# Starting the first layer norm inside the output projection, slice by slice, in a post-norm transformer layer on 8 cores

## The chip, the cores and the metric

The kernel runs on all 8 cores of one Trainium2 chip. Every core runs the same program on its own data (half of the tokens of one of four sequences) and nothing is exchanged between cores. The metric is the device time in microseconds of the slowest core. TensorE is the matrix engine (PE in the profile, PEld its weight loads), VectorE is DVE, ScalarE is ACT, GpSimd is POOL, SyncE is SP.

## The reference

One transformer layer with layer norms after the residual sums:

```
x = layernorm(x + attention(x, Wq, Wk, Wv, Wo))        # causal, 16 heads of 64, D = 1024
x = layernorm(x + down(silu(gate(x)) * up(x)))         # hidden 3072, int weights / 127
layernorm(v) = (v - mean(v)) / sqrt(var(v) + 1e-5)     # over the 1024 features
```

The input is 4 sequences of 4096 tokens with 1024 features in float32.

## The kernel before

Each core owns 2048 tokens (`TOWN`). Activations lie transposed: the 1024 features are `NCH` = 8 chunks of 128 partitions, the tokens are columns. `y` is the float32 tile of 128 x (8 x 2048) that holds the residual stream. Work on it goes by *slice* `s` (`NQS` = 4 slices of 512 tokens) and by chunk (`ncx` or `m`, 0 to 7).

The kernel has stages one after the other: attention with its projections; the output projection Wo; the first layer norm; the feed-forward part; the second layer norm; one store of `y`. A barrier of all engines stands behind attention, behind the first layer norm and behind the second.

**Output projection.** A list `wo_iters` has 32 entries (chunk outside, slice inside). For each, TensorE runs 8 matmuls of 128x512 (line 642) into one of two PSUM tiles `wps`, and VectorE adds the residual `xres` and writes `y` (line 649, called the eviction here). The matmuls of an entry wait until the eviction two entries back has emptied their tile. SyncE loads `xres` four entries ahead. Behind the list TensorE and ScalarE wait for the last eviction, the PSUM of the projection is given back and that of the layer norm is taken: `stp`, two pairs of 1x512 sums, and `bc2`, two pairs of 128x512 broadcasts.

**Layer norm** (`ln_stats_and_apply`, used for both norms). `stats(s)` does for each chunk a Square on ScalarE (line 555, y to bf16 `ysq`), a cast on VectorE (line 559, y to bf16 `ybf`) and two matmuls against a column of ones (lines 563 and 565), which add the sums over features into `stp`. `ysq` and `ybf` have two buffers each. Behind that, for each slice, comes a chain on one-partition rows: Square on ScalarE (579), variance on VectorE (583), Ln and Exp on ScalarE (587, 590), the shift on VectorE (593), then float32 matmuls that spread scale and shift over 128 partitions into `bc2` (598, 600). Then the *apply*: 8 multiplications and 8 additions on VectorE (607, 609), in place in `y`. `stats(0)` and `stats(1)` go first; `stats(s + 2)` is issued behind the apply of slice s, and its matmuls wait for it, since both use the same `stp` pair.

Every engine takes its instructions in the order in which the program issues them, so the order of these calls is the order on each engine. What matters of it here is, in the projection, the wait of the matmuls for `wps`, and in the layer norm:

```
for s in range(min(2, NQS)):
    stats(s)
for s in range(NQS):
    ...chain and apply of slice s...
    if s + 2 < NQS:
        stats(s + 2)
```

Of the kernel before, what the change touches and what calls it, by code (L numbers as in the profile page):

```python
# [8 lines left out]
F32 = mybir.dt.float32  # L9
# [4 lines left out]
ALU = mybir.AluOpType  # L14
# [17 lines left out]
class Sem:  # L32
    def __init__(self, stack, nc, name):
        self.h = stack.enter_context(nc.semaphore(name))
        self.n = 0
# [7 lines left out]
def build_program(cfg):  # L43
    D, NH, DH, HID, T = cfg["D"], cfg["NH"], cfg["DH"], cfg["HID"], cfg["T"]
    NCH = D // 128
    NHC = HID // 128
    NB = T // 128
    TOWN = T // 2
    NBANK = TOWN // 512
    NKVS = T // 512  # L50
    NQS = TOWN // 512
# [8 lines left out]
    nc = bass.Bass("TRN2", target_bir_lowering=False, num_devices=1)  # L60
# [22 lines left out]
    with st:  # L83
        consts = st.enter_context(nc.sbuf_tensor("consts", [128, 4], F32))
        ones_col_bf = st.enter_context(nc.sbuf_tensor("ones_col_bf", [128, 1], BF16))
        ones_row_f = st.enter_context(nc.sbuf_tensor("ones_row_f", [1, 128], F32))
# [12 lines left out]
        s_evV = Sem(st, nc, "s_evV")  # L99
# [16 lines left out]
        s_lnA = Sem(st, nc, "s_lnA")  # L116
        s_lnV = Sem(st, nc, "s_lnV")
        s_lnP = Sem(st, nc, "s_lnP")
# [397 lines left out]
        if debug:  # L516
# [4 lines left out]
        y = st.enter_context(nc.sbuf_tensor("y", [128, NCH * TOWN], F32))  # L521
# [7 lines left out]
        ysq = [ph_b.enter_context(nc.sbuf_tensor(f"ysq{i}", [128, 512], BF16))  # L529
               for i in range(2)]  # L530
        ybf = [ph_b.enter_context(nc.sbuf_tensor(f"ybf{i}", [128, 512], BF16))
               for i in range(2)]
        rows = ph_b.enter_context(nc.sbuf_tensor("rows", [1, 6 * 512], F32))
# [3 lines left out]
            woT.rearrange("(c p) n -> p c n", p=128)), 16)  # L537
        wo_ready = s_wo.n

        def ln_stats_and_apply(stp, bc2, ysq, ybf, rows, sA, sV, sP):  # L540
            ysq_free = [0, 0]
            ybf_free = [0, 0]
            stats_done = [0, 0]
            bc_done = [0, 0]
            apply_done = [0, 0]
            rows_free = 0

            def stats(s):
                sb = s % 2
                q0 = s * 512  # L550
                nc.tensor.wait_ge(sV.h, apply_done[sb])
                for m in range(NCH):
                    bi = m % 2
                    nc.scalar.wait_ge(sP.h, ysq_free[bi])
                    sA.inc(nc.scalar.activation(  # L555
                        ysq[bi][:, :], y[:, m * TOWN + q0: m * TOWN + q0 + 512],
                        AF.Square))
                    nc.vector.wait_ge(sP.h, ybf_free[bi])
                    sV.inc(nc.vector.tensor_copy(
                        ybf[bi][:, :], y[:, m * TOWN + q0: m * TOWN + q0 + 512]))  # L560
                    nc.tensor.wait_ge(sA.h, sA.n)
                    nc.tensor.wait_ge(sV.h, sV.n)
                    nc.tensor.matmul(stp[sb][0][:, :], ones_col_bf[:, :], ybf[bi][:, :],  # L563
                                     start=(m == 0), stop=(m == NCH - 1))
                    sP.inc(nc.tensor.matmul(  # L565
                        stp[sb][1][:, :], ones_col_bf[:, :], ysq[bi][:, :],
                        start=(m == 0), stop=(m == NCH - 1)))
                    ysq_free[bi] = sP.n
                    ybf_free[bi] = sP.n
                stats_done[sb] = sP.n  # L570

            for s in range(min(2, NQS)):
                stats(s)
            for s in range(NQS):
                sb = s % 2
                q0 = s * 512
                nc.scalar.wait_ge(sP.h, stats_done[sb])
                nc.scalar.wait_ge(sP.h, rows_free)
                sA.inc(nc.scalar.activation(rows[:, 0:512], stp[sb][0][:, :],
                                            AF.Square, scale=1.0 / D))  # L580
                nc.vector.wait_ge(sA.h, sA.n)
                nc.vector.wait_ge(sP.h, stats_done[sb])
                sV.inc(nc.vector.scalar_tensor_tensor(  # L583
                    rows[:, 1536:2048], stp[sb][1][:, :], 1.0 / D, rows[:, 0:512],
                    op0=ALU.mult, op1=ALU.subtract))
                nc.scalar.wait_ge(sV.h, sV.n)
                sA.inc(nc.scalar.activation(rows[:, 2048:2560], rows[:, 1536:2048],
                                            AF.Ln, bias=float(cfg["EPS"])))
                nc.scalar.wait_ge(sA.h, sA.n)
                sA.inc(nc.scalar.activation(rows[:, 2048:2560], rows[:, 2048:2560],  # L590
                                            AF.Exp, scale=-0.5))
                nc.vector.wait_ge(sA.h, sA.n)
                sV.inc(nc.vector.scalar_tensor_tensor(  # L593
                    rows[:, 2560:3072], stp[sb][0][:, :], -1.0 / D, rows[:, 2048:2560],
                    op0=ALU.mult, op1=ALU.mult))
                nc.tensor.wait_ge(sV.h, sV.n)
                nc.tensor.wait_ge(sV.h, apply_done[sb])
                nc.tensor.matmul(bc2[sb][0][:, :], ones_row_f[:, :], rows[:, 2048:2560],  # L598
                                 start=True, stop=True)
                sP.inc(nc.tensor.matmul(bc2[sb][1][:, :], ones_row_f[:, :],  # L600
                                        rows[:, 2560:3072], start=True, stop=True))
                bc_done[sb] = sP.n
                rows_free = sP.n
                nc.vector.wait_ge(sP.h, bc_done[sb])
                for m in range(NCH):
                    yv = y[:, m * TOWN + q0: m * TOWN + q0 + 512]
                    sV.inc(nc.vector.tensor_mul(yv, yv, bc2[sb][0][:, :]))  # L607
                    nc.vector.wait_ge(sV.h, sV.n)
                    sV.inc(nc.vector.tensor_add(yv, yv, bc2[sb][1][:, :]))  # L609
                apply_done[sb] = sV.n  # L610
                if s + 2 < NQS:
                    stats(s + 2)
            nc.tensor.wait_ge(sV.h, sV.n)
            nc.scalar.wait_ge(sV.h, sV.n)

        wo_iters = [(ncx, s) for ncx in range(NCH) for s in range(NQS)]
        wps_free = [0, 0]
        xr_free = [0, 0, 0, 0]
        xr_done = [0, 0, 0, 0]
# [13 lines left out]
        for idx, (ncx, s) in enumerate(wo_iters):  # L633
            q0 = s * 512
            i = idx % 2
            j = idx % 4
# [4 lines left out]
            for kcx in range(NCH):  # L641
# [3 lines left out]
                    start=(kcx == 0), stop=(kcx == NCH - 1))  # L645
# [6 lines left out]
            xr_free[j] = s_evV.n  # L652
            if idx + 4 < len(wo_iters):
                issue_xres(idx + 4)
        nc.tensor.wait_ge(s_evV.h, s_evV.n)
        nc.scalar.wait_ge(s_evV.h, s_evV.n)
        ofm_st.close()
        wo_ps.close()
        ln_ps = ExitStack()
        stp = [[ln_ps.enter_context(nc.psum_tensor(f"stp{i}_{j}", [1, 512], F32))  # L660
                for j in range(2)] for i in range(2)]
        bc2 = [[ln_ps.enter_context(nc.psum_tensor(f"bc2{i}_{j}", [128, 512], F32))
                for j in range(2)] for i in range(2)]
        ln_stats_and_apply(stp, bc2, ysq, ybf, rows, s_lnA, s_lnV, s_lnP)
        ln_ps.close()
        ph_b.close()
        nc.all_engine_barrier()
        if debug:
# [35 lines left out]
        for fs in range(NFS):  # L704
# [11 lines left out]
            for hc in range(NHC):  # L716
# [12 lines left out]
                for nh in range(NH2):  # L729
# [3 lines left out]
                    for m in range(NCH):  # L733
# [3 lines left out]
                            start=(m == 0), stop=(m == NCH - 1))  # L737
# [4 lines left out]
                    for m in range(NCH):  # L742
# [3 lines left out]
                            start=(m == 0), stop=(m == NCH - 1))  # L746
# [16 lines left out]
            for dc in range(NCH):  # L763
                for nh in range(NH2):
                    c0 = nh * 512
                    i = (dc * NH2 + nh) % 2
                    nc.tensor.wait_ge(s_fdve.h, dps_free[i])
                    last = None
                    for hc in range(NHC):
# [3 lines left out]
                            start=(hc == 0), stop=(hc == NHC - 1))  # L773
                    s_fpe.inc(last)
                    nc.vector.wait_ge(s_fpe.h, s_fpe.n)
                    yv = y[:, dc * TOWN + t0 + c0: dc * TOWN + t0 + c0 + 512]
                    s_fdve.inc(nc.vector.scalar_tensor_tensor(
                        yv, dps[i][:, :], cfg["QSCALE"], yv,
                        op0=ALU.mult, op1=ALU.add))
# [6 lines left out]
        stpc = [[ln_ps2.enter_context(nc.psum_tensor(f"stc{i}_{j}", [1, 512], F32))  # L786
                 for j in range(2)] for i in range(2)]
        bcc = [[ln_ps2.enter_context(nc.psum_tensor(f"bcc{i}_{j}", [128, 512], F32))
                for j in range(2)] for i in range(2)]
        ysq2 = [ph_c.enter_context(nc.sbuf_tensor(f"ysq2{i}", [128, 512], BF16))  # L790
                for i in range(2)]
        ybf2 = [ph_c.enter_context(nc.sbuf_tensor(f"ybf2{i}", [128, 512], BF16))
                for i in range(2)]
        rows2 = ph_c.enter_context(nc.sbuf_tensor("rows2", [1, 6 * 512], F32))
        ln_stats_and_apply(stpc, bcc, ysq2, ybf2, rows2, s_lnA, s_lnV, s_lnP)
        ln_ps2.close()
        ph_c.close()
        nc.all_engine_barrier()
# [66 lines left out]
```

## Time and profile before

| | us |
|---|---|
| median of 2 runs (2127.88 to 2134.34) | 2131.11 |
| the profiled execution, its time | 2126.39 |
| its span, slowest core (core 4) | 2125.3 |
| spans of the 8 cores | 2107.4 to 2125.3 |
| mean granted TensorE clock of the cores | 0.844 to 0.852 of full |

Busy time in the span of 2125.3 us: TensorE 1614.1 us (76%), ScalarE 797.8 us (38%), VectorE 641.1 us (30%), GpSimd 162.4 us (8%). How to read the rows of a timeline: start in us, duration in us (of the whole merged stretch where a count above 1 stands behind), engine, line, operation, output from input, count, and in brackets how long the engine was idle before and which instruction released it. PEclk is the granted TensorE clock as a share of 2.4 GHz; 0.50 is 1.2 GHz.

### The profile page before, as it was taken

The page shows a single profiled execution, that of the slowest core. Times are in us where ns is not written, and L with a number is a line of the kernel's source. Part 1 is how long each engine was busy: PE and PEld are TensorE (multiplying, and loading weights), DVE is VectorE, ACT ScalarE, POOL GpSimd, SP SyncE. Part 2 cuts the span into 40 slices and gives each one's busy share as a digit, 9 for nine tenths or more (in the row PEclk, how much of TensorE's full clock was granted, in tenths as well). Part 3 has the DMA queues.
Part 4 walks back from the last instruction along what each step waited for, and adds up shares of the span by engine and source line. Part 5 has one row for each costly group of instructions (what it writes and reads, how often), then busy time and mean ns, then how long its engine had stood idle before and what let it go on. Part 6 is the DMA issues. An engine that isn't in the chain of part 4 may idle for free. (4 is left out here: it accounts for less than half of the span.)

```text
span 2125.3 us, 22768 instructions; the slowest of 8 cores (2107.4 to 2125.3 us)
## 1 busy us (share of the span) xinstructions
PE 1614.1 (76%) x7146; PEld 618.6 (29%) x7240; DVE 641.1 (30%) x1500; ACT 797.8 (38%) x935; POOL 162.4 (8%) x205
## 2 busy tenths in 40 slices
PE   3858988789887788885776749524699989999830
PEld 1513333133332233321211114101244434444300
DVE  1333242532423533325213123562111121111254
ACT  0025766667663566644485810310111001110220
POOL 1010000000001000010000010002122002220000
PEclk9968999789996799975696859857899999999965
DMA  7791324523250622320000025008878207870004
GB/s 100 109 129 21 54 47 60 67 44 60 41 80 3 88 43 41 61 41 3 1 1 1 1 49 137 15 0 113 95 70 80 21 0 70 80 70 1 1 0 158
DMA packets 173633, 109.02 MB, mean 51 GB/s; under 512 B 102574, under 2 KB 164016, under 8 KB 172496
## 3 DMA queue, kind: packets, MB, share of 16 engines
q0 software_dynamic: 167744, 90.65, 33.2%
q1 hardware_dynamic: 5776, 16.91, 2.6%
q8 instruction: 65, 1.06, 0.2%
q14 instruction: 48, 0.39, 0.1%
HBM read 189.07 MB, written 8.65 MB: 93 GB/s over the span
## 5 line engine op out<-in xcount | busy, mean ns | idle before, releaser
L415 ACT ACTIVATE pt<-sp,cbias 128x1024 bf16<-128x1024 f32 (+3 forms) x640 | 622.6, 985 | 364.9 <-PE sp L403 353.6
L443 PE MATMUL op<-pt,vbuf 128*65 128x512 bf16 (+3 forms) x1280 | 378.7, 381 | 124.9 <-DVE pt L424 55.3
L398 PE MATMUL sp<-qbuf,kbuf 64*128 64x512 bf16 (+3 forms) x640 | 239.4, 383 | 2.1 <-DVE cbias L324 2.1
L403 PE MATMUL sp<-qbuf,kbuf 64*128 64x512 bf16 (+3 forms) x640 | 239.6, 383 | 0.0
L734 PE MATMUL gps<-x1b,wgb 128*128 128x512 bf16 x752 | 185.8, 388 | 65.1 <-DMA wub<-wuT 57.2
L751 ACT ACTIVATE sgb<-gps 128x512 bf16<-128x512 f32 x96 | 57.3, 597 | 420.8 <-PE gps L734 420.8
L443 PEld LDWEIGHTS op<-pt,vbuf 128*65 128x65 bf16 x1280 | 121.8, 117 | 267.6 <-issue 224.2
L743 PE MATMUL ups<-x1b,wub 128*128 128x512 bf16 x753 | 182.8, 384 | 0.8
L226 PE MATMUL pp<-xstg,wkb 128*128 128x512 bf16 x481 | 145.4, 416 | 45.6 <-DMA xstg<-xfm 40.0
L770 PE MATMUL dps<-hbuf,wdb 128*128 128x512 bf16 x752 | 165.2, 379 | 3.1 <-DVE hbuf L755 2.3
L240 PE MATMUL pp<-wvb,xstg 128*128 128x256 bf16 x1024 | 163.2, 280 | 0.6
L755 DVE TENSOR_TENSOR hbuf<-sgb,ups 128x512 bf16<-128x512 bf16 x96 | 66.0, 688 | 319.9 <-PE ups L743 319.9
L398 PEld LDWEIGHTS sp<-qbuf,kbuf 64*128 64x128 bf16 x640 | 58.4, 94 | 252.5 <-issue 250.4
L734 PEld LDWEIGHTS gps<-x1b,wgb 128*128 128x128 bf16 x768 | 74.1, 99 | 164.9 <-issue 84.4
L555 ACT ACTIVATE ysq<-y 128x512 bf16<-128x512 f32 x64 | 38.6, 625 | 179.4 <-DVE y L649 104.3
L421 DVE TENSOR_TENSOR pt<-pt,mka 128x128 bf16<-128x128 bf16 x128 | 28.7, 224 | 249.7 <-ACT pt L415 248.2
L743 PEld LDWEIGHTS ups<-x1b,wub 128*128 128x128 bf16 x768 | 76.1, 99 | 94.0 <-issue 5.8
L770 PEld LDWEIGHTS dps<-hbuf,wdb 128*128 128x128 bf16 x768 | 74.9, 98 | 93.4 <-issue 3.2
L297 ACT ACTIVATE qsq<-kbuf 128x512 bf16<-128x512 bf16 x64 | 39.5, 627 | 161.4 <-DVE qbuf L272 138.9
L240 PEld LDWEIGHTS pp<-wvb,xstg 128*128 128x128 bf16 x1024 | 81.2, 98 | 59.0 <-issue 43.9
L252 DVE CAST vbuf<-pp 128x256 bf16<-128x256 f32 x128 | 54.4, 425 | 138.9 <-PE pp L240 138.3
L264 PE MATMUL pp<-xstg,wqb 128*128 128x512 bf16 x246 | 74.1, 420 | 24.7 <-DMA xstg<-xq 24.1
(89 smaller groups left out, 1187.3 us busy)
## 6 DMA issues: line engine op xcount, KB each, us to landing
xstg<-xfm POOLq DMA_DIRECT2D x32, 1024.0 KB, 9.1
xstg<-xq POOLq DMA_DIRECT2D x16, 1024.0 KB, 8.4
wgb<-wgT POOLq DMA_DIRECT2D x48, 256.0 KB, 4.5
wub<-wuT POOLq DMA_DIRECT2D x48, 256.0 KB, 5.3
xres<-xq SPq DMA_DIRECT2D x32, 256.0 KB, 3.8
yout<-y SPq DMA_DIRECT2D x1, 8192.0 KB, 23.4
wdb<-wdT POOLq DMA_DIRECT2D x1, 6144.0 KB, 44.2
wqb<-wqT POOLq DMA_DIRECT2D x4, 512.0 KB, 7.7
```

The source lines that it names most:

```text
L226: return nc.tensor.matmul(ps[:, 0:512], wkb[pb][:, m * PD + nk * 128: m * PD + nk * 128 + 128], xs[:, m * 512:(m + 1) * 512], start=(m == ...
L240: return nc.tensor.matmul(ps[:, 0:PD], xs[:, m * 512 + jb * 128: m * 512 + jb * 128 + 128], wvb[pb][:, m * PD:(m + 1) * PD], start=(m == 0 ...
L264: return nc.tensor.matmul(ps[:, 0:512], wqb[pb][:, m * PD + nq * 128: m * PD + nq * 128 + 128], xs[:, m * 512:(m + 1) * 512], start=(m == ...
L398: nc.tensor.matmul(sp[buf][:, js * 128: 512], kbuf[pb][0:64, hp * T + kb * 128: hp * T + kb * 128 + 128], qbuf[pb][0:64, hp * TOWN + qbase ...
L403: s_s.inc(nc.tensor.matmul(sp[buf][:, 512 + js * 128: 1024], kbuf[pb][64:128, hp * T + kb * 128: hp * T + kb * 128 + 128], qbuf[pb][64:128 ...
L415: s_exp.inc(nc.scalar.activation(pview, sview, AF.Exp, bias=cbias[pb][:, 0:1]))
L443: lastpv = nc.tensor.matmul(ops[hl][:, js * 128: 512], vbuf[pb][:, kb * VGW + (2 * hp + hl) * 65: kb * VGW + (2 * hp + hl) * 65 + 65], pt[ ...
L734: lastg = nc.tensor.matmul(gps[:, :], wgb[wi][:, m * 128:(m + 1) * 128], x1b[:, m * FFS + c0: m * FFS + c0 + 512], start=(m == 0), stop=(m ...
L743: last = nc.tensor.matmul(ups[:, :], wub[wi][:, m * 128:(m + 1) * 128], x1b[:, m * FFS + c0: m * FFS + c0 + 512], start=(m == 0), stop=(m ...
L751: s_fact.inc(nc.scalar.activation(sgb[:, :], gps[:, :], AF.Silu))
L755: s_fdve.inc(nc.vector.tensor_mul(hbuf[:, hc * FFS + c0: hc * FFS + c0 + 512], sgb[:, :], ups[:, :]))
L770: last = nc.tensor.matmul(dps[i][:, :], wdb[:, hc * D + dc * 128: hc * D + dc * 128 + 128], hbuf[:, hc * FFS + c0: hc * FFS + c0 + 512], s ...
```

## The change

The layer norm helper becomes a class `LN` with two methods, `stats(s)` and `finish(s)` (the chain and the apply of one slice), so that its calls can be placed among other work.

- The list of the output projection now has the slice outside and the chunk inside. When the 8 chunks of slice s are done, the program issues `stats(s)` and, from s = 1 on, `finish(s - 1)`; behind the list comes `finish(3)`.
- The PSUM of the first layer norm is taken ahead of the projection, beside `wps`: two `stp` pairs as before, but one `bc2` pair in place of two. The waits for a free `stp` and a free `bc2` are kept apart (`apply_st`, `apply_bc`).
- In `stats`, ScalarE waits for the slice's last eviction (`ready_of`).
- In `stats`, in both layer norms, the cast to `ybf` goes from VectorE to ScalarE (`nc.scalar.copy`), behind the Square of the same chunk.
- The second layer norm has the old order of calls, written out, and both its `bc` pairs.

```diff
             def stats(self, s):
-                nc.tensor.wait_ge(sV.h, apply_done[sb])
+                nc.tensor.wait_ge(sV.h, self.apply_st[sb])
+                if self.ready_of is not None:
+                    sem, val = self.ready_of(s)
+                    nc.scalar.wait_ge(sem.h, val)
                 for m in range(NCH):
                     bi = m % 2
...
-                    nc.vector.wait_ge(sP.h, ybf_free[bi])
-                    sV.inc(nc.vector.tensor_copy(
-                        ybf[bi][:, :], y[:, m * TOWN + q0: m * TOWN + q0 + 512]))
+                    nc.scalar.wait_ge(sP.h, self.ybf_free[bi])
+                    sA.inc(nc.scalar.copy(
+                        self.ybf[bi][:, :], y[:, m * TOWN + q0: m * TOWN + q0 + 512]))
                     nc.tensor.wait_ge(sA.h, sA.n)
-                    nc.tensor.wait_ge(sV.h, sV.n)
...
+        bc2 = [[ln_ps.enter_context(nc.psum_tensor(f"bc2{i}_{j}", [128, 512], F32))
+                for j in range(2)] for i in range(1)]
...
-        wo_iters = [(ncx, s) for ncx in range(NCH) for s in range(NQS)]
+        wo_iters = [(ncx, s) for s in range(NQS) for ncx in range(NCH)]
...
             if idx + 4 < len(wo_iters):
                 issue_xres(idx + 4)
-        nc.tensor.wait_ge(s_evV.h, s_evV.n)
-        nc.scalar.wait_ge(s_evV.h, s_evV.n)
+            if ncx == NCH - 1:
+                y_slice_done[s] = s_evV.n
+                ln1.stats(s)
+                if s >= 1:
+                    ln1.finish(s - 1)
+        ln1.finish(NQS - 1)
...
+        ln2 = LN(stpc, bcc, ysq2, ybf2, rows2, s_lnA, s_lnV, s_lnP)
+        for s in range(min(2, NQS)):
+            ln2.stats(s)
+        for s in range(NQS):
+            ln2.finish(s)
+            if s + 2 < NQS:
+                ln2.stats(s + 2)
```

## Rows read from the trace of the kernel before

**Rows 1.** Stages by windows: us, busy (instructions) of each engine, PEclk, DMA share, GB/s

```profile
1279.60:1337.20 57.60, 56.49 (x250) 25.24 (x254) 22.08 (x33) 0.00 (x0) 0.00 (x0) 0.97 0.51 128
1337.20:1436.40 99.20, 35.22 (x80) 7.79 (x80) 60.00 (x105) 25.91 (x44) 0.00 (x0) 0.64 0.00 0
...
2002.00:2101.50 99.50, 35.23 (x80) 7.59 (x80) 60.07 (x105) 27.63 (x45) 0.00 (x0) 0.64 0.00 0
```

**Rows 2.** Groups by line, 1279.6 to 1437 us: busy, mean ns, idle before, releaser

```profile
L649 DVE TENSOR_TENSOR y<-wps,xres 128x512 f32<-128x512 f32 x32 | 22.1, 692 | 53.2 <-PE wps L642 53.2
...
L555 ACT ACTIVATE ysq<-y 128x512 bf16<-128x512 f32 x32 | 19.1, 624 | 141.8 <-DVE y L649 104.3 <-PE stp L565 37.4
```

**Rows 3.** Timeline, evictions 8 and 32, and the first stats operations behind the last

```profile
1295.13 0.69 DVE L649 TENSOR_TENSOR y<-wps,xres 128x512 f32<-128x512 f32 x1 [1.04 <-PE wps L642]
...
1336.57 0.69 DVE L649 TENSOR_TENSOR y<-wps,xres 128x512 f32<-128x512 f32 x1 [1.03 <-PE wps L642]
1337.18 0.75 DVE L559 CAST ybf<-y 128x512 bf16<-128x512 f32 x2
1337.41 1.15 ACT L555 ACTIVATE ysq<-y 128x512 bf16<-128x512 f32 x2 [104.29 <-DVE y L649]
...
1338.29 0.38 PE L563 MATMUL stp<-ybf,ones_col_bf 128*1 128x512 bf16 x1 [1.90 <-ACT ysq L555]
...
1338.50 0.38 PE L565 MATMUL stp<-ysq,ones_col_bf 128*1 128x512 bf16 x1
...
1338.98 1.15 ACT L555 ACTIVATE ysq<-y 128x512 bf16<-128x512 f32 x2 [0.42 <-PE stp L565]
```

**Rows 4.** Timeline, slice 0: its chain, its apply and the apply's end

```profile
1349.48 0.57 ACT L579 ACTIVATE rows<-stp 1x512 f32<-1x512 f32 x1
...
1350.23 0.68 DVE L583 SCALAR_TENSOR_TENSOR rows<-stp,rows 1x512 f32<-1x512 f32 x1 [0.85 <-ACT rows L579]
...
1354.32 1.76 PE L600 MATMUL bc<-rows,ones_row_f 1*128 1x512 f32 x2
...
1356.19 0.69 DVE L607 TENSOR_TENSOR y<-y,bc 128x512 f32<-128x512 f32 x1 [3.06 <-PE bc L600]
...
1367.31 0.76 DVE L559 CAST ybf<-y 128x512 bf16<-128x512 f32 x2
```

**Rows 5.** TensorE in 4 us windows: us, busy (instructions), PEclk, DMA share, GB/s

```profile
1280.00:1284.00 4.00, 4.00 (x14) 0.65 0.00 0
1284.00:1288.00 4.00, 4.00 (x20) 1.00 0.43 85
...
1352.00:1356.00 4.00, 2.62 (x4) 0.81 0.00 0
...
1368.00:1372.00 4.00, 3.72 (x9) 0.56 0.00 0
```

**Rows 6.** Timeline, slices 1 and 3 of the first layer norm

```profile
1366.71 0.69 DVE L609 TENSOR_TENSOR y<-y,bc 128x512 f32<-128x512 f32 x1
...
1373.89 0.57 ACT L579 ACTIVATE rows<-stp 1x512 f32<-1x512 f32 x1
...
1418.16 0.67 DVE L583 SCALAR_TENSOR_TENSOR rows<-stp,rows 1x512 f32<-1x512 f32 x1
...
1425.16 0.69 DVE L607 TENSOR_TENSOR y<-y,bc 128x512 f32<-128x512 f32 x1 [4.11 <-PE bc L600]
...
1435.68 0.69 DVE L609 TENSOR_TENSOR y<-y,bc 128x512 f32<-128x512 f32 x1
```

**Rows 7.** Timeline, the second layer norm: first Square, first row operation, first apply

```profile
2003.51 1.15 ACT L555 ACTIVATE ysq<-y 128x512 bf16<-128x512 f32 x2
...
2016.38 0.57 ACT L579 ACTIVATE rows<-stc 1x512 f32<-1x512 f32 x1
...
2024.13 0.69 DVE L607 TENSOR_TENSOR y<-y,bcc 128x512 f32<-128x512 f32 x1 [4.11 <-PE bcc L600]
```

**Rows 8.** One line's instructions: the loads of activation tables

```profile
L28 ACT ACT_TABLE_LOAD  x3: 1283/1283/1283, 1.1 to 2002.2; - x3
```

## What was predicted before the changed kernel ran

> **What bounds the kernel now.** I read the page first (TensorE is busy for three quarters of the span), then the busy time by stage, and then only the two stages that the change touches, in the groups by line and the timeline. The reader is to see three things. The projection with its evictions lasts 57 us and TensorE is busy nearly all of it [rows 1]; the evictions wait for matmuls 53.2 us of it [rows 2]. They come every (1336.57 - 1295.13) / 24 = 1.727 us [rows 3], a group of eight matmuls at 2.4 GHz. The two layer norms last 99 us each, and no engine is busy for more than 60 of them [rows 1]: they are chains through three engines. And TensorE's clock: it is at the upper level while Wo runs, at 1.2 GHz in the first microseconds of it, when TensorE had been idle before, and it falls again when TensorE has little to do in the layer norm [rows 5]. The aim of such an overlap would be to run the norm's 99 us under the projection. VectorE has the room. The question is the order on TensorE.
>
> **Part 1, the slice boundary.** All engines take the calls in order, so the next slice's Wo matmuls stand on TensorE's queue behind `stats(s)` and, from s = 1, behind the broadcast matmuls of `finish(s - 1)`. TensorE itself waits at each boundary.
>
> - From the last eviction's start to the first Square: 1337.41 - 1336.57 = 0.84 us [rows 3].
> - Square and copy now alternate on ScalarE. No row has the copy; I price it as a Square. Two of these take 1.15 us [rows 3], one 0.63 [rows 2], so the second starts 0.52 behind the first, and a chunk costs 1.04. With two buffers, chunk m + 2 also waits for chunk m's matmuls: 1.15 for both operations, 0.25 until the matmul (1338.29 behind a Square's end at 1337.41 + 0.63), 0.21 + 0.38 for both matmuls, 0.10 to the next Square (1338.98) [rows 3]: 2.09 us for two chunks, about the same as ScalarE's own 2.08. At 1.2 GHz both matmuls take 1.05 in place of 0.59: 2.55 us.
> - Eight chunks up to the next free place on ScalarE: 3 x 2.09 + 2.08 = 8.35 us, or 3 x 2.55 + 2.08 = 9.7. I take 9.0. TensorE is free after 6.27 + 1.04 + 1.15 + 0.25 + 0.43 = 9.1 us, or 10.9. I take 10.0, in the middle, since TensorE is busy for 0.43 of 1.04 us here, and rows show either clock beside such shares [rows 5].
> - From the row Square to the first apply operation: 1356.19 - 1349.48 = 6.7 us [rows 4], 2024.13 - 2016.38 = 7.75 at 1.2 GHz [rows 7]. I take 7.2. The broadcast ends as the apply begins (1354.32 + 1.76 = 1356.08) [rows 4], so TensorE is held as long.
>
> **Part 2, Wo behind an apply.** For slices 2 and 3 VectorE has an apply in its queue ahead of the evictions: 1367.31 - 1356.19 = 11.1 us [rows 4]. TensorE can fill its two `wps` tiles in 3.5 us, or 6.9 at 1.2 GHz, and then stands until the first eviction is over. I take 11.1, then 0.9 (an eviction of 0.69 [rows 2] and a handover of 0.2), a third group at 1.2 GHz with its last matmul 3.0 us behind its first, five groups at 1.727 (8.6), and 0.57 to its eviction: 24.2 us from the first apply operation to the slice's last eviction. Without the apply ahead (slice 1) it is 7 x 1.727 + 2.1 = 14.2, plus 1.7 for one group at half clock, 15.9.
>
> **The sum of projection and first norm**, starts in the clock of the profiled execution:
>
> - last eviction of slice 0 at 1295.1 [rows 3], Square at 1296.0, TensorE free at 1306.0;
> - last eviction of slice 1 at 1321.8, Square 1322.7, rows of slice 0 at 1331.7, apply(0) from 1338.9;
> - last eviction of slice 2 at 1363.1, Square 1363.9, rows 1372.9, apply(1) from 1380.1;
> - last eviction of slice 3 at 1404.3, Square 1405.2, rows 1414.2, apply(2) from 1421.4;
> - `finish(3)`: its variance stands behind apply(2) on VectorE as it does now: 1421.4 + 11.1 = 1432.5, then 7.0 to the apply (1425.16 - 1418.16) and 11.2 for it (1435.68 + 0.69 - 1425.16) [rows 6]: 1450.7.
>
> It now ends at 1436.4, so this part costs 14.4 us more. With every unknown at 2.4 GHz (9.1, 8.35, 6.7, no slow group, 6.0 in `finish(3)` by 1356.19 - 1350.23 [rows 4]) it ends at 1440.7, +4.3. With all at 1.2 GHz (10.9, 9.7, 7.8, two slow groups behind an apply) it ends at 1458.9, +22.5. The order of the `xres` loads costs nothing: they are of the same size, four entries ahead, and an entry never gets shorter. The single `bc2` pair costs nothing: the broadcast of slice s always comes behind the apply of s - 1 by the order on VectorE.
>
> **Part 3, the second norm.** Only the copies move. The first 16 chunks now take 2016.38 - 2003.51 = 12.9 us [rows 7]; with both operations on ScalarE 7 x 2.09 + 2.08 = 16.7, or 19.9 at 1.2 GHz: +3.8 to +7.1, I take 5.4. For slices 2 and 3 two chunks lie ready before the apply ends, but the other six do not: from the apply's end (1366.71 + 0.69) to the row Square it is now 6.5 us [rows 6], the same in both norms; with the change 1.4 to the third Square, then 2 x 2.09 + 2.08: 7.6, or 8.5. That is +1.1 to +2.0, I take 1.6, twice. The second norm: +8.6, bounds +6.1 and +11.2.
>
> The copy goes to the slower engine: two casts on VectorE take 0.75 us, one starting about 0.32 behind the other, against 0.52 on ScalarE [rows 3], and VectorE is idle in exactly these stretches. The Trainium skill, "ScalarE: Activation LUTs", section "Rules for kernel authors", speaks against such a move too: it gives simple elementwise work to VectorE. By it, with the casts left on VectorE, the second norm would add nothing and the first would save 32 x (1.04 - 0.75), 9 us, where 0.75 is a chunk now, (1349.48 - 1337.41) / 16 [rows 3, 4]; the sum would be some 18 us lower than mine, near 2132.
>
> **Everything else** is untouched, and all 8 cores do the same. The feed-forward part starts its weight loads behind the barrier, so it moves as a block.
>
> **The sum.** 14.4 + 8.6 = +23.0 us on the profiled execution's 2126.4: 2149.4 us. The median of the two runs is 4.7 us above the profiled one. I say 2150. Bounds: +10.4 and +33.7, so 2136.8 to 2160.1.
>
> **Rivals.**
>
> 1. *TensorE's order does not bind* (faster). If the next slice's Wo matmuls ran while the stats matmuls wait, the projection would end at 1336.6 as now, with the applies of slices 0 and 1 in VectorE's gaps, and behind it would come 0.8 + 9.0 + 7.2 + 11.1 + 7.0 + 11.2 = 46 us: 1383, 53 earlier, with the second norm's +8.6 a time of 2082. It decides if more than two thirds of TensorE's waits at the boundaries vanish. Against it: no row shows a matmul ahead of one issued before it. Chance 1%.
> 2. *TensorE never gets back to full clock in slices 1 to 3* (slower). 24 groups at 3.45 in place of 1.727 us are 41 us, of which I count 5: +36, 2186. Against it: in Wo's first 4 us the clock rose while TensorE was fully busy [rows 5]. Chance 3%. The Trainium skill, "TensorE: Matmul & The Clock Gate", section "Part 1: The HAM clock gate", says likewise that sustained activity releases the throttle.
> 3. *The copy is dearer than a Square.* At 1.0 us (double) it adds 0.48 x 64 on the path, 31 us: 2181, slower by 2.3%. No row prices it. The Trainium skill, "ScalarE: Activation LUTs", section "What ACT_TABLE_LOAD costs", gives all functions one speed. Chance 3%.
> 4. *Copy and Square need different tables.* A load is 1.28 us [rows 8]; 64 copies with two loads each are 164 us: 2314. Against it: Square, Ln and Exp follow each other now with three loads in the whole kernel [rows 8]. Chance 1%.
> 5. *No difference or a little faster* (below 2131): the stats stretches keep the clock and the handovers overlap better than priced. It needs more than 20 of my 23 us to be wrong, beyond my lower bounds. Chance 6%.
>
> **How the numbers follow.** My forecast has 86%. The range 2134 to 2166 holds the bounds, with 3 us of scatter below (the two runs stand 3.2 us either side of their median) and the median's 4.7 above. Within 2% of 2131 (43 us, about what a measurement of this kernel can tell from no change) lie the forecast and rival 5 and half of rival 3: 93%. Slower by over 2%: rivals 2, 4 and half of 3, with a little for what I have not seen: 5%. Faster: rival 1 and as much again: 2%.
>
> **What the profile after would show.** Evictions in four blocks of eight, with gaps near 10 us behind the first, and near 17 us behind the second and third before TensorE's next Wo matmul; then a second gap, the third eviction group waiting on VectorE's apply; TensorE's idle time before stats matmuls released by ScalarE; the first norm's last addition ending near 1451; the second norm near 107 us long; the copy near 0.6 us with no table load beside it. A copy of another duration, Wo matmuls between the stats matmuls, or a clock that stays up in all stats stretches would make the prediction wrong.

## The result

| | before | changed |
|---|---|---|
| median of all executions | 2129.4 us (10) | 2158.6 us (12) |
| median without those left out (next sentence) | 2127.9 us (8) | 2154.0 us (9) |
| ratio to before, 95% interval | | 1.0133 (1.0107 to 1.0158) |
| profiled execution, span of the slowest core | 2125.3 us | 2152.9 us (core 5) |

Executions in which a die showed a lower granted clock are left out of all ratios and of every time that is called measured below, and of the profiled execution of experiment 1, where it befell cores 0 to 3, only cores 4 to 7 are used. The change costs 28 us by the ratio, 1.3%: a real loss, and within the 2% that were called no change.

The next table is the one to compare kernels by. It holds means over the eight cores of one profiled execution each, cut at four events: the first Wo matmul, the first operation of the feed-forward part (`x1b`), the load of the activation table ahead of the second norm, and the issue of the store.

| us, mean of 8 cores | up to Wo | Wo and first norm | feed-forward | second norm | store |
|---|---|---|---|---|---|
| before | 1268.5 | 158.4 | 565.0 | 101.3 | 23.5 |
| changed | 1268.8 | 171.8 | 568.8 | 112.0 | 23.3 |
| difference | +0.3 | +13.4 | +3.8 | +10.7 | -0.2 |

So the two stages that the change touches account for 24 of the 28 us. The two stages in the slowest core of the changed kernel, by windows (us, busy time and instructions of TensorE, its weight loads, VectorE, ScalarE and GpSimd, then TensorE's clock, DMA share, GB/s), answering [rows 1]:

```profile
1273.40:1443.10 169.70, 102.74 (x336) 35.38 (x336) 68.55 (x104) 40.91 (x76) 0.00 (x0) 0.76 0.15 44
...
2017.50:2128.20 110.70, 42.87 (x80) 8.19 (x80) 46.80 (x72) 42.85 (x77) 0.00 (x0) 0.57 0.00 0
```

In the second norm TensorE's busy time rose from 35.2 us [rows 1] to 42.9 for the same 80 matmuls, and its mean clock fell from 0.64 to 0.57 of full. That is the first sign of what the prediction had mis-sized. Now the first boundary, from the timeline of the same core. Line 668 is the eviction, 567 and 571 the Square and the copy, 574 and 577 the stats matmuls, 661 Wo's (before: 649, 555, 559, 563, 565, 642):

```profile
1289.81 0.69 DVE L668 TENSOR_TENSOR y<-wps,xres 128x512 f32<-128x512 f32 x1 [1.03 <-PE wps L661]
1290.65 0.63 ACT L567 ACTIVATE ysq<-y 128x512 bf16<-128x512 f32 x1 [65.78 <-DVE y L668]
1291.18 0.60 ACT L571 CAST ybf<-y 128x512 bf16<-128x512 f32 x1
...
1291.93 0.38 PE L574 MATMUL stp<-ybf,ones_col_bf 128*1 128x512 bf16 x1 [2.30 <-ACT ybf L571]
...
1292.14 0.38 PE L577 MATMUL stp<-ysq,ones_col_bf 128*1 128x512 bf16 x1
1292.22 0.60 ACT L571 CAST ybf<-y 128x512 bf16<-128x512 f32 x1
...
1292.97 0.38 PE L574 MATMUL stp<-ybf,ones_col_bf 128*1 128x512 bf16 x1 [0.45 <-ACT ybf L571]
...
1299.41 0.38 PE L577 MATMUL stp<-ysq,ones_col_bf 128*1 128x512 bf16 x1
...
1299.72 13.99 PE L661 MATMUL wps<-ofm,wob 128*128 128x512 bf16 x64
```

The eviction of slice 0's last chunk starts at 1289.81. The Square follows 0.84 us later, as in [rows 3], and then each chunk comes 1.04 us behind the other (matmuls at 1291.93, 1292.97), with TensorE waiting for the copy. TensorE gets the next Wo matmul at 1299.72, 9.07 us behind the Square. All that time the projection of slice 1 stood behind matmuls that were waiting. Core 5 is among the quickest here: over the eight cores it is 9.1 to 10.4 us, 9.7 in the mean, because on five of them TensorE's clock fell during these stats. The same 16 matmuls in core 0 and in core 5 (core 0 first; us, busy time and count of TensorE, clock, DMA share, GB/s):

```profile
1284.70:1293.10 8.40, 6.56 (x16) 0.64 0.08 26
```

```profile
1291.90:1299.50 7.60, 4.45 (x16) 1.00 0.12 32
```

Then the place where VectorE's queue holds the projection (rows of 592 and 611 are the chain, 620 the apply):

```profile
1323.04 0.58 ACT L592 ACTIVATE rows<-stp 1x512 f32<-1x512 f32 x1
...
1326.96 2.04 PE L611 MATMUL bc<-rows,ones_row_f 1*128 1x512 f32 x2 [3.09 <-DVE rows L606]
...
1328.80 1.91 PE L613 MATMUL bc<-rows,ones_row_f 1*128 1x512 f32 x2
...
1330.64 6.25 PE L661 MATMUL wps<-ofm,wob 128*128 128x512 bf16 x16
1330.81 0.69 DVE L620 TENSOR_TENSOR y<-y,bc 128x512 f32<-128x512 f32 x1 [4.11 <-PE bc L613]
...
1341.93 1.28 DVE L668 TENSOR_TENSOR y<-wps,xres 128x512 f32<-128x512 f32 x2
...
1342.77 12.21 PE L661 MATMUL wps<-ofm,wob 128*128 128x512 bf16 x48 [5.88 <-DVE y L668]
...
1355.16 0.69 DVE L668 TENSOR_TENSOR y<-wps,xres 128x512 f32<-128x512 f32 x1 [1.03 <-PE wps L661]
```

From the row Square (1323.04) to the first apply operation (1330.81) are 7.8 us, of which the broadcast's matmuls (1326.96, 1328.80) take 3.8 at 1.2 GHz; then 16 matmuls of Wo fill both PSUM tiles (1330.64), and TensorE is idle for 5.88 us until VectorE has finished the apply and emptied a tile (1341.93, 1342.77). The last eviction of the slice starts 24.35 us behind the first apply operation (24.7 in the mean of the eight cores). The tail of the first norm and the second norm (line 592 the row Square, 596 its variance, 622 the addition):

```profile
1424.93 0.67 DVE L596 SCALAR_TENSOR_TENSOR rows<-stp,rows 1x512 f32<-1x512 f32 x1
...
1431.93 0.69 DVE L620 TENSOR_TENSOR y<-y,bc 128x512 f32<-128x512 f32 x1 [4.11 <-PE bc L613]
...
1442.45 0.69 DVE L622 TENSOR_TENSOR y<-y,bc 128x512 f32<-128x512 f32 x1
```

```profile
2018.79 0.63 ACT L567 ACTIVATE ysq<-y 128x512 bf16<-128x512 f32 x1
...
2023.77 0.58 PE L574 MATMUL stc<-ybf,ones_col_bf 128*1 128x512 bf16 x1
...
2023.84 0.63 ACT L567 ACTIVATE ysq<-y 128x512 bf16<-128x512 f32 x1 [0.21 <-PE stc L577]
2024.15 0.63 PE L577 MATMUL stc<-ysq,ones_col_bf 128*1 128x512 bf16 x1
...
2037.86 0.58 ACT L592 ACTIVATE rows<-stc 1x512 f32<-1x512 f32 x1
...
2044.84 0.69 DVE L620 TENSOR_TENSOR y<-y,bcc 128x512 f32<-128x512 f32 x1 [3.33 <-PE bcc L613]
```

In the second norm TensorE runs at 1.2 GHz from the first matmul pair on: the second of two starts 0.38 us behind the first, not 0.21. The ScalarE Square waits for it (`PE stc L577`). The first 16 chunks take 2037.86 - 2018.79 = 19.1 us. The clock by windows of 4 us:

```profile
2016.00:2020.00 4.00, 0.62 (x3) 0.83 0.00 0
2020.00:2024.00 4.00, 3.26 (x7) 0.50 0.01 2
...
2032.00:2036.00 4.00, 3.32 (x8) 0.53 0.00 0
2036.00:2040.00 4.00, 1.48 (x6) 1.00 0.00 0
```

It falls behind 3.5 us in which TensorE had nothing to run until the first copy was there, and then stays at 1.2 GHz for some 15 us. So it is on all eight cores: between the first and the last stats matmul of slice 0 the mean clock is 0.50 to 0.54 of full. In the first norm, behind Wo and a gap of 2.3 us, the same 16 matmuls kept the upper level on three cores.

### The profile page after: what moved, and what is told of

Its sections match the earlier page's. It is cut to its first block and busy times, and to the rows that moved or that the text cites. A ratio compares the mean times of both kernels' runs of the same rounds, so it can differ in the third digit from the quotient of the medians.

```text
span 2152.9 us, 22801 instructions; the slowest of 8 cores (2136.6 to 2152.9 us)
## 1 busy us (share of the span) xinstructions
PE 1635.4 (76%) x7240; PEld 619.6 (29%) x7240; DVE 614.6 (29%) x1436; ACT 828.7 (38%) x999; POOL 162.4 (8%) x205
```

## The experiments

**1. The casts back on VectorE, the new order kept.**

```diff
-                    nc.scalar.wait_ge(sP.h, self.ybf_free[bi])
-                    sA.inc(nc.scalar.copy(
+                    nc.vector.wait_ge(sP.h, self.ybf_free[bi])
+                    sV.inc(nc.vector.tensor_copy(
                         self.ybf[bi][:, :], y[:, m * TOWN + q0: m * TOWN + q0 + 512]))
                     nc.tensor.wait_ge(sA.h, sA.n)
+                    nc.tensor.wait_ge(sV.h, sV.n)
```

> The changed kernel with the casts of both layer norms back on VectorE; the new order of calls stays. Theory A (two separate costs: TensorE waiting at the slice boundaries, and copies on ScalarE): the second norm is back to 99 us (from 111), and in the first a chunk costs 0.79 in place of 1.04 us, four slices of eight, 8 us: 171 becomes about 163. Together 20 us below the changed kernel: 2139, still 8 to 10 us above before. Theory B (the whole loss is the copies, the order costs nothing): no slower than before, 2129 or less.

Measured: 2125.7 us, ratio to before 1.000 (0.998 to 1.002). The projection and first norm take 159.3 us and the second norm 102.5. That is theory B: the order of calls alone costs nothing that can be told from noise (+0.9 us in its stage, where theory A had 8 to 10 on the whole), and the copies cost 12.5 us in the first norm and about 10 in the second. The timeline of a slice in core 4 shows it:

```profile
1312.78 0.69 DVE L669 TENSOR_TENSOR y<-wps,xres 128x512 f32<-128x512 f32 x1 [1.03 <-PE wps L662]
1313.39 0.75 DVE L571 CAST ybf<-y 128x512 bf16<-128x512 f32 x2
1313.62 1.15 ACT L567 ACTIVATE ysq<-y 128x512 bf16<-128x512 f32 x2 [15.78 <-DVE y L669]
...
1320.56 0.57 ACT L593 ACTIVATE rows<-stp 1x512 f32<-1x512 f32 x1
...
1328.31 0.69 DVE L621 TENSOR_TENSOR y<-y,bc 128x512 f32<-128x512 f32 x1 [4.11 <-PE bc L614]
```

From the Square to the row Square are 6.9 us here and 5.8 and 6.1 in the next two slices (1353.49 to 1359.29 and 1391.32 to 1397.39); with the copies on ScalarE they were 8.3, 8.3 and 8.9 in core 5, and 8.7 each in the mean of the eight cores. The two casts start on VectorE ahead of the Square, since they stand behind the eviction on the same engine.

**2. The kernel before with the casts on ScalarE.**

```diff
-                    nc.vector.wait_ge(sP.h, ybf_free[bi])
-                    sV.inc(nc.vector.tensor_copy(
+                    nc.scalar.wait_ge(sP.h, ybf_free[bi])
+                    sA.inc(nc.scalar.copy(
                         ybf[bi][:, :], y[:, m * TOWN + q0: m * TOWN + q0 + 512]))
                     nc.tensor.wait_ge(sA.h, sA.n)
-                    nc.tensor.wait_ge(sV.h, sV.n)
```

> The kernel before with only the casts of both norms moved to ScalarE. Theory A: each norm pays what the second norm paid in the changed kernel, 11 us: 22 above before, 2152. Rival (the second norm's 11 us come from something else in the changed kernel, such as its place in time or TensorE's clock history): the norms stay near 99 us and the time within 5 us of before.

Measured: 2146.7 us, ratio 1.0114 (1.0096 to 1.0131). Projection and first norm 167.9 (+9.5), second norm 111.4 (+10.1), as expected. One edit of the change carries nearly all of the loss, in either order. The copy itself is no dearer than I priced it (groups by line of core 5, first norm; beside it the VectorE cast is 426 ns in the kernel before):

```profile
L555 ACT ACTIVATE ysq<-y 128x512 bf16<-128x512 f32 x32 | 20.0, 625 | 139.5 <-DVE y L648 108.3 <-PE stp L564 31.2
L559 ACT CAST ybf<-y 128x512 bf16<-128x512 f32 x32 | 19.2, 601 | 0.0
```

**3. What the 10 us of the second norm are.** This kernel is the changed one, with matmuls added in the second norm that only keep TensorE at work (besides those named below, 12 ahead of the first chunk); their result goes to an unused tile. The single broadcast pair in the second norm makes room for it.

```diff
+            def keep(self, n):
+                if self.warm is not None:
+                    for _ in range(n):
+                        nc.tensor.matmul(self.warm[:, :], self.wsrc[:, 0:128],
+                                         self.wsrc[:, 0:512], start=True, stop=True)
```

> The changed kernel, with matmuls whose result nobody reads put into the second norm (two behind each chunk, 12 in each wait for the row chain, 48 in each apply), into a PSUM tile that the single broadcast pair leaves free. It keeps TensorE at work and takes nothing from the others. If the second norm's extra time beyond the pure ScalarE pace is TensorE at 1.2 GHz: the first 16 chunks go from 19.1 to 16.7 us, each of three chains from 7.0 to 7.8 down to 6.7, the last from 7.0 to 6.0, the other stats from 8 to 7.6; the norm from 112 to about 105. Rival (ScalarE sets the pace in all of it): the norm stays at 112, or grows where the extra matmuls delay those that are needed.

Measured: 2140.3 us, ratio to before 1.0056 (1.0029 to 1.0082), against 1.0133 for the changed kernel. The second norm takes 103.1 us, 8.9 less, with every copy still on ScalarE; the rest of the difference lies in stages that the edit leaves alone (up to Wo, feed-forward). The window of it and the chain of its first slice:

```profile
2011.10:2113.40 102.30, 98.47 (x396) 33.78 (x396) 46.83 (x72) 42.31 (x77) 0.00 (x0) 0.98 0.00 1
```

```profile
2012.42 0.63 ACT L574 ACTIVATE ysq<-y 128x512 bf16<-128x512 f32 x1
...
2029.51 0.58 ACT L600 ACTIVATE rows<-stc 1x512 f32<-1x512 f32 x1
...
2033.55 1.12 PE L620 MATMUL bcc<-rows,ones_row_f 1*128 1x512 f32 x2
2034.51 1.02 PE L622 MATMUL bcc<-rows,ones_row_f 1*128 1x512 f32 x2
...
2035.63 0.69 DVE L630 TENSOR_TENSOR y<-y,bcc 128x512 f32<-128x512 f32 x1 [2.47 <-PE bcc L622]
```

The clock is at 0.98 of full. The edit has a cost of its own: the 48 matmuls behind the last broadcast end 1.0 us behind the last apply, and the store is issued 1.35 us behind that apply in place of 0.38 (means of 8 cores). 16 chunks take 17.1 us, not 19.1, and from the row Square to the apply 6.1, where it was 7.0 in this place and 7.8 in the other two. Read alone, this would put four fifths of the second norm's 10.7 us on the clock. It can't be read alone: the kernel before also spends much of its norm at 1.2 GHz, and the next experiment is the control.

**4. The same in the kernel before** (old order, casts on VectorE), in both norms: 12 extra matmuls ahead of the first chunk, one behind each chunk, 12 in each wait for the chain, 48 in each of the first three applies; here too one broadcast pair in place of two.

```diff
                     ybf_free[bi] = sP.n
+                    keep(1)
...
+                keep(12)
                 nc.tensor.wait_ge(sV.h, sV.n)
...
                 rows_free = sP.n
+                keep(48 if s + 1 < NQS else 0)
```

> The kernel before (old order, casts on VectorE) with matmuls whose result nobody reads in both layer norms: one behind each chunk, 12 in each wait for the row chain, 48 in each of the first three applies; the broadcast has one PSUM pair in place of two. If TensorE's clock is part of what the norms cost in the kernel before too, then each norm loses what 1.2 GHz adds: about 1 us in each of four row chains and broadcasts, 1 us in each of two later stats and 1 in the first: 101 becomes 94, both norms together 14 us less, a ratio to before of 0.993. Rival (with the casts on VectorE the clock is up often enough, the extra matmuls only stand in the way): no change or up to 5 us more.

Measured: 2120.5 us, ratio 0.9945 (0.991 to 0.998). The first norm's stage is 153.8 us (-4.6), the second norm 95.2 (-6.1), a little less than the 14 together that I expected; its window in core 4 has the clock at 0.95:

```profile
1980.60:2075.60 95.00, 78.39 (x310) 27.89 (x316) 59.82 (x104) 27.89 (x45) 0.00 (x0) 0.95 0.00 1
```

Now the two norms can be set beside each other with the clock up in both. From the first Square to the end of the last apply, which leaves out the late matmuls of experiment 3, they take (means of 8 cores) 100.5 us with the copies on ScalarE and 93.5 with them on VectorE; without the extra matmuls it is 110.3 and 99.7. So about 7 us of the second norm's 10.6 are ScalarE's pace, and 3 to 4 are what the slower filling adds by way of the clock. The split is rough: the two kernels have two extra matmuls a chunk and one, and clocks of 0.98 and 0.95. In the slowest cores, which show where these lie, the changed kernel against the one before has +6.2 us in the first 16 chunks (19.07 and 12.87), +3.0 from the apply's end to the row Square in two slices, and +2.2 in the four chains; in the means of the eight cores these are +5.9, +3.3 and +1.4.

**5. Taking TensorE's waits away.** In the changed kernel, the stats of slice s - 1 are spread between the groups of slice s; chain and apply stay a block.

```diff
+            if s >= 1:
+                ln1.act_chunk(s - 1, ncx)
...
+            if s >= 1 and ncx >= 1:
+                ln1.pe_chunk(s - 1, ncx - 1)
             if ncx == NCH - 1:
                 y_slice_done[s] = s_evV.n
-                ln1.stats(s)
                 if s >= 1:
+                    ln1.pe_chunk(s - 1, NCH - 1)
                     ln1.finish(s - 1)
+        ln1.stats(NQS - 1)
         ln1.finish(NQS - 1)
```

> The changed kernel, with the stats of slice s - 1 spread chunk by chunk between the projection's groups of slice s, so that TensorE has a group of 1.7 us to do while ScalarE makes the next chunk; chain and apply stay one block behind a slice. Theory A: three boundary waits of 8 to 10 us become 8 x 0.43 us of matmuls; projection and first norm together 171 becomes 137, the time 2124. Rival (the stage is bound by the sum of the norm's own chains, whatever TensorE does): it stays above 160, the time above 2147.

Measured: 2127.1 us, ratio 1.0007 (0.999 to 1.003). The stage takes 144.7 us, 27 less than in the changed kernel, where I expected 34; the second norm keeps its 111.5.

**6. Chain and apply spread as well**: the chain of slice s - 2 goes to the first groups of slice s, its broadcast behind the fifth, and its apply, one chunk behind each eviction, over the last three groups of slice s and the first five of the next.

```diff
+            if s >= 2 and ncx == 0:
+                ln1.row_var(s - 2)
+            if s >= 2 and ncx == 1:
+                ln1.row_shift(s - 2)
+            if s >= 3 and ncx <= 4:
+                ln1.apply(s - 3, ncx + 3)
+            if s >= 2 and ncx == 4:
+                ln1.bcast(s - 2)
+            if s >= 2 and ncx >= 5:
+                ln1.apply(s - 2, ncx - 5)
```

> As the one with the stats between the groups, but the chain of slice s - 2 and its apply (one chunk behind an eviction) are spread over the projection too, and the last slice's broadcast goes to the projection's free PSUM tiles. Theory A: three blocks at TensorE's pace, 17 to 20 us each, behind a first of 15, and a tail of 32: about 105 us for projection and first norm (158 before, 171 in the changed kernel), the time 2092. Rival (VectorE, with evictions, applies and chain in one queue, becomes the bound and holds the evictions): over 125 us, the time above 2112.

Measured: 2103.3 us, ratio 0.991 (0.988 to 0.994). The stage takes 120.4 us: 51 less than in the changed kernel and 38 less than before, and 15 more than I expected. Part of the miss stands in core 3's timeline (739 the Wo matmuls, 580 and 583 the stats, 746 the evictions, 682 and 684 the broadcast, 698 the apply's addition):

```profile
1330.62 0.38 PE L580 MATMUL stp<-ybf,ones_col_bf 128*1 128x512 bf16 x1
...
1330.84 0.38 PE L583 MATMUL stp<-ysq,ones_col_bf 128*1 128x512 bf16 x1
...
1331.14 1.90 PE L739 MATMUL wps<-ofm,wob 128*128 128x512 bf16 x8
...
1332.97 0.38 PE L580 MATMUL stp<-ybf,ones_col_bf 128*1 128x512 bf16 x1
...
1337.24 0.69 DVE L698 TENSOR_TENSOR y<-y,bc 128x512 f32<-128x512 f32 x1
...
1338.18 1.55 PE L682 MATMUL bc<-rows,ones_row_f 1*128 1x512 f32 x2 [2.26 <-DVE y L698]
...
1339.52 1.91 PE L684 MATMUL bc<-rows,ones_row_f 1*128 1x512 f32 x2
...
1341.36 3.59 PE L739 MATMUL wps<-ofm,wob 128*128 128x512 bf16 x8
```

A group with its stats pair takes 1332.97 - 1330.62 = 2.35 us, not the 1.73 + 0.43 that I had counted. With one `bc2` pair, the broadcast also waits for the last addition of the apply before (1337.24 to 1338.18), and what comes behind it runs at 1.2 GHz: 3.6 us for a Wo group. The Wo groups spread over 79.8 us, where I had 73; the tail is 40.6, where I had 32 (means of 8 cores).

**7. The casts of the second norm back on VectorE in that kernel**, those of the first left on ScalarE, since VectorE has evictions and applies in its queue there.

```diff
         ln2 = LN(stpc, bcc, ysq2, ybf2, rows2, s_lnA, s_lnV, s_lnP)
+        ln2.cast_v = True
```

> The kernel with stats, chain and apply spread over the projection, with one more edit: the casts of the second norm back on VectorE, those of the first stay on ScalarE, where VectorE has the evictions and applies to do. Theory A: the second norm goes from 111 to 101 us and the first keeps its 120: 10 us less, a ratio to before of 0.986. Rival (that the second norm's 10 us belong to a slower clock of TensorE that stays whatever is done): no gain.

Measured: 2088.1 us, ratio 0.982, with a wide interval (0.972 to 0.992). The stages say it better: 120.3 and 101.2 us, so the second norm gives 10.2 back and the first keeps its time.

**8. The second norm of slices 0 and 1 under the second half of the feed-forward part**, with the early store of their output. `it` counts the 48 iterations of gate and up.

```diff
+                    for ls in range(2):
+                        if 0 <= it - 10 * ls < NCH:
+                            ln2a.act_chunk(ls, it - 10 * ls)
...
+                        if 0 <= it - 10 * ls < NCH:
+                            ln2a.pe_chunk(ls, it - 10 * ls)
+                        if it - 10 * ls == 10:
+                            ln2a.bcast(ls)
...
+                        if 0 <= it - 10 * ls - 11 < NCH:
+                            ln2a.apply(ls, it - 10 * ls - 11)
```

> The same idea carried on from the kernel with the split casts: the second norm of slices 0 and 1, final after the first half of the feed-forward part, runs one chunk per iteration among the gate and up groups of the second half, and their half of the output is stored there. By the order theory only what TensorE itself runs is paid: 32 matmuls and two broadcasts, some 15 us in that stage, while the second norm behind it goes from 101 to about 51 us and the store from 23 to 12: 47 us less than with the split casts, a ratio to before of 0.965. Rival (the early store takes the DMA time of the weight loads, or ScalarE's four table loads hold the silus up): the stage grows by 40 us or more and the gain is under 25 us.

Measured: 2068.0 us, ratio 0.969 (0.966 to 0.972). Second norm and store together went from 124 to 63 us, as expected. But the feed-forward stage grew by 38 us (565.5 to 603.8), where I had 15, so that the stages together give about 22 us and not 47, near the rival's under 25. Of the 38, 16 are longer waits for `wub` (58 to 74 us in the means of 8 cores). The waits between 1725 and 1960 us in core 1, the second half of that part (engine, what waited, for whom: total, times, longest), are below; in the kernel of experiment 7 the slowest core waits 0.8 us for `wub` there:

```profile
PE gps L920 <- DMA wub<-wuT: 17.8, 7, 13.2
...
PE stc L591 <- DVE ybf L573: 6.1, 6, 1.0
```

**9. The early store moved to the down projection**, where no weights are loaded.

```diff
-                    if 30 <= it < 30 + NCH:
-                        m0 = it - 30
...
+                if fs == 1:
+                    nc.sync.wait_ge(s_lnV.h, ln2a.apply_bc[0])
+                    nc.sync.wait_ge(s_fpe.h, s_fpe.n)
+                    s_out.inc(nc.sync.dma_start(
+                        yout[dc * 128:(dc + 1) * 128, 0:FFS],
+                        y[:, dc * TOWN: dc * TOWN + FFS]), 16)
```

> The kernel with slices 0 and 1 of the second norm under the feed-forward part, with one edit: their store goes out chunk by chunk among the down projection's groups, when no weights are being loaded, in place of the gate and up iterations 30 to 37. If the early store took DMA time from the weight loads, the 14 to 16 us by which TensorE waits longer for them are gone and the ratio to before falls from 0.969 to about 0.962. Rival (the longer waits for weights have another cause): no change.

Measured: 2053.1 us, ratio 0.962 (0.954 to 0.970). The feed-forward stage fell to 587.8 us and the waits for `wub` to 59.7, where they had been without the early store; casts and applies stayed where they were, so it was the store that lengthened them. The stage is still 22 us longer than in experiment 7, 7 more than I had; no run takes that apart. This is the fastest version, 80 us under its runs of before.

## Why the prediction was right, and where its steps were not

It said 2150 with a range of 2134 to 2166 and 93% for within 2%; measured were 2158.6 (2154.0 in the second row of the table) and 1.33%. Its sum was +23.0 on the profiled execution; the two stages show +24.1, and 3.8 more stand in the feed-forward part. Numbers of cores are of the profiled executions.

- **TensorE waits at each boundary.** Right: 0.84 to the Square, 1.04 a chunk, and TensorE free after 9.1 to 10.4 us, 9.7 in the mean of the eight cores, where I had 10.0 between bounds of 9.1 and 10.9. From a Square to the row Square it was 8.3 to 9.3, mean 8.7, where I had 9.0. That the clock would be up in some of these stretches and down in others was right too.
- **Wo behind an apply.** 24.35 us measured in core 5, 24.7 and 24.6 in the means for slices 2 and 3, 24.2 counted. The slow group that I gave slice 1, where no apply stands ahead, did not come: 14.3 us from its first matmul to its last eviction, where the sum has 15.9. The last chain, 7.0 us (1424.93 to 1431.93), and the last apply came as in [rows 6].
- **The sum of projection and first norm.** +13.4 us measured as a mean over cores, +14.4 counted. But its parts were not what I thought, and that their errors cancel is luck. The kernel with the order alone has +0.9 us, and mine implied 14.4 - 9 = 5.4 for it; the move of the cast cost 12.5, and I had 9. Set beside each other (means of the changed kernel's eight cores and of cores 4 to 7 of experiment 1), the move made the four stretches of stats 3.1, 1.8, 2.9 and 2.4 us longer, 10.3 in all: the first from the Square to the next Wo matmul (9.7 against 6.6), the others from the Square to the row Square (8.7 against 6.9, 5.8 and 6.3). So the price of a chunk was near right. The rest is what I had at nothing for the cast: two of the three chains behind them are 0.6 us longer each (7.8 against 7.2 and 7.1), and about 1 us stands in the Wo groups. In slice 0 the clock was at full level through the stats on each of the cores 4 to 7 with the casts on VectorE, as on all eight of the kernel before, and on three of eight with the copies on ScalarE. Of the 4.5 us too many for the order, 1.2 are the base: I started from core 4, whose stage took 157.2 us before, and the mean is 158.4. The rest is the clock, which I had at the lower level for a group of slice 1 (1.7 us) and between the levels in the stats; in experiment 1 it was at full through slice 0's stats and the groups behind them.
- **The second norm.** +8.6 counted with an upper bound of 11.2; +10.7 measured. The first 16 chunks took 19.1 us, near my slow bound of 19.9, and the later slices 7.9 and 8.2 in place of 6.5, inside 7.6 to 8.5. What I left out is that the chains behind them slow down too: in [rows 7] and its like the slowest core of the kernel before has one chain at 7.75 us and two near 6.3; that of the changed kernel has two at 7.8 and one at 7.0. They make 2.2 us there, and 1.4 in the means of the eight cores, the larger part of a miss of 2.1. Experiments 3 and 4 agree: at full clock the move costs about 7 us, and the clock adds 3 to 4. I had put the clock in the middle between two bounds in each stretch of stats, and at no cost in the chains behind.
- **The clock.** Extra matmuls alone took 8.9 us off the second norm of the changed kernel and 6.1 off that of the kernel before, at 0.98 and 0.95 of full clock (experiments 3 and 4). The Trainium skill, "TensorE: Matmul & The Clock Gate", section "Part 1: The HAM clock gate", says that activity releases the throttle and idleness brings it back; the traces agree.
- **The rule that spoke against the change.** With the casts on VectorE and the new order, measured are 2125.7 us, a ratio of 1.000 to before, where I had put 2132 (experiment 1). The Trainium skill, "ScalarE: Activation LUTs", section "Rules for kernel authors", gives simple elementwise work such as additions and multiplications to VectorE; for this cast the trace agrees (426 ns on VectorE, 601 on ScalarE). Whether it holds in the spread order, where VectorE has evictions and applies in its queue, was not tried: experiments 6 and 7 both leave the casts of the first norm on ScalarE.
- **The rivals.** No matmul of Wo passed one that waited (rival 1). Wo's groups came back to 1.73 us each (rival 2). The copy takes 601 ns against 625 for the Square, with three table loads as before (rivals 3 and 4).
- **What stays open.** The feed-forward part was 3.8 us longer in the profiled execution of the changed kernel, all of it on cores 4 to 7, in waits for `wub`. Experiment 3 has the same order of work up to there and 565.7 us. I take it for scatter between executions, but it wasn't tried apart.

So the forecast was right mostly for its own reasons, and in part by luck. The new order by itself is neutral, and what made the kernel slower is the cast, in either order. That the order is neutral because TensorE's waits give back what it hides is supported by experiments 5 and 6, where the stage loses 27 and 51 us once they are gone.

## What to carry to other kernels

Placing a stage's calls inside another stage does not overlap them when the engine that both need takes its instructions in order (159.3 us against 158.4 here): spread the pieces so that each waiting matmul has a group of useful ones ahead of it (171.8 to 120.4 us). Price a move to another engine together with what stands behind it, the chain and the matmuls at the lower clock, and run the control at the same clock before blaming the clock. A stretch of short matmuls between waits may be worth filling with matmuls for nobody (4.6 and 6.1 us in the two norms of the kernel before), but not so many that they outlast the work beside them (1.0 us in experiment 3). An early store belongs where no weights are being loaded (15 us of the time here).

## What was not expected of the hardware

The same 16 stats matmuls behind the same Wo matmuls and the same gap of 2.30 us ran at 2.4 GHz throughout on cores 3, 4 and 5 of the changed kernel, and with a mean clock of 0.51 to 0.80 of full on the other five, in one execution. With the casts on VectorE, in the kernel before, the gap was 1.9 us, a chunk took 0.75 us and not 1.04, and the clock was at full on all eight. Behind the down projection and a gap of 3.45 us it was 0.50 to 0.54 on all eight cores. So neither the gap nor the work around it settles the clock of one core's stretch; what else does, no run here shows, and one core's trace is not enough to tell.

Also, going from 128-wide weights to one-column weights and back cost 0.2 us for each pair: a group of eight and a pair took 2.35 us, where 10 matmuls of 0.216 make 2.16. The matmul behind the pair started 0.31 us after it and not 0.21 (1331.14 behind 1330.84), and in experiment 3 the extra matmul, which waits for nothing, did so too.
